# Two packs of weighted values behind one another in every second score step of an attention kernel

## The chip, the core and the metric

The kernel runs on one core of a Trainium2 chip. Five engines work side by side and meet through semaphores: TensorE (PE in the profile; its weight loads are listed apart as PEld), VectorE (DVE), ScalarE (ACT), GpSimd (POOL) and SyncE (SP), which issues nearly all DMAs here. The metric is the device time of one execution in microseconds. The kernel before takes 1724.98 us (median of 3 runs, 1724.56 to 1728.42).

## What is computed

Eight batches, each with 512 query rows of 256 values, attend to a context of 1601 rows (16 heads of 16 values), and then pass a gated feed-forward net whose inputs and weights are rounded blockwise to a four-bit format.

```python
def attention(query, key, value):             # per batch: query 512 x 256, key = value 1601 x 256
    q = split_heads(query @ Wq.T + bq)        # 16 heads of 16
    k = split_heads(key @ Wk.T + bk)
    v = split_heads(value @ Wv.T + bv)
    attn = softmax(einsum('bhqd,bhkd->bhqk', q, k) / sqrt(16))
    return merge_heads(einsum('bhqk,bhkd->bhqd', attn, v)) @ Wo.T + bo
x = x + attention(layernorm(x), ctx, ctx)
xn = layernorm(x)
h = silu(fp4(xn) @ fp4(w_gate).T) * (fp4(xn) @ fp4(w_up).T)      # 704 wide
x = x + fp4(h) @ fp4(w_down).T
```

## The kernel before

The program is one long pipeline over the batches. An iteration computes the attention of one batch (part "att"), the projections and row maxima of the next batch ("early"), the feed-forward net of the batch before ("late"), and loads for the one after that ("next"). There is a prologue, a "first" iteration without a late part, six "loop" iterations, a "last" iteration without an early part, and a tail that holds only a late part.

An iteration has 52 steps: 4 groups of 4 heads times 13 tiles of up to 128 context rows. Step n computes, for the four heads of its group, the scores of one context tile against all 512 queries. The order on every engine is written out by hand, and every engine runs its own list in order. On TensorE a step is, in this order:

- the scores of heads 0 and 1 (`scores(n, 0)`, L837, tile `st`): two bf16 matmuls of 512 columns;
- one "shared" job from the table SLOTS, in the bank `misc`: v (values of a context tile, L720, with the transposes of a tile of the next context, L808), k and q (projections of keys and queries, L713 and L699), o (output projection, L799), xnT, xqT and hqT (transposes), gate and up (L758), down0 and down (L771 and L779). In a loop iteration every step has one;
- the scores of heads 2 and 3;
- two pairs of products of queries and keys for the row maxima (L856, tile `mx`, on 48 of the array's rows each), which VectorE reduces (L1120);
- in some steps a second job (nm, xqT or hqT);
- the weighted values of the step before (`weighted(n - 1)`, L871, tile `pvb`): four fp32 products with 32 columns of weights each, one per head, next to each other in the array. The trace has two rows for each, so a pack is eight rows, in two rounds of four.

ScalarE turns the scores into softmax weights, in the same order: the exponentials of heads 0 and 1 (L1042, tile `prob`), what its engine has to do for the shared job (copying v and the context tile, biases of k or q, tanh for gate, the copies of the transposes), the exponentials of heads 2 and 3, and the copy of a second job.

Three limits matter for the change. Scores have two PSUM banks in a loop iteration: heads 0 and 2 use one, heads 1 and 3 the other. So a score of head 0 of step n+1 waits until the exponential of head 2 of step n has read its bank, and head 1 waits for head 3 (`exp_done2` and `exp_done3`; the class ScoreBanks). In a first or last iteration, steps without a shared job use `misc` as a third bank, and the last one has two more from step 35 on. `prob` has two places, used by turns, so the exponentials of step n wait until `weighted(n - 2)` is done (`pv_done`). And the accumulation in `pvb` runs over the 13 steps of a group; ScalarE then copies it to `pvs` (L1047) at the end of steps 13, 26 and 39 and of step 0 of the next iteration.

Of the kernel before, what the change touches and what calls it, by code (L numbers as in the profile page):

```python
# [5 lines left out]
BF16 = mybir.dt.bfloat16  # L6
# [9 lines left out]
NKT = 13  # L16
# [5 lines left out]
HG = 4  # L22
# [185 lines left out]
LINKS = {"early": 13, "late": 43}  # L208


class Iteration:


# [60 lines left out]
def xattn_ffn(nc, x, ctx_in, wqT, wkT, wvT, woT, bq, bk, bv, bo, w_gate, w_up, w_down, out, scr_k, scr_q):  # L274
    es = ExitStack()
    with es:
# [19 lines left out]
        kp = cin[:, 0:3 * TP // 2].bitcast(BF16).rearrange("p (a n) -> p a n", a=3)  # L296
        kx = [cin[:, 3 * TP // 2 + 402 * j:3 * TP // 2 + 402 * j + 401] for j in range(2)]
        ctxT = sb("ctxT", [128, NC2, TP])
        qp = sb("qp", [128, 3, S], BF16)
        qx = sb("qx", [128, S])  # L300
        kstack = sb("kstack", [ROWS, H, TP], BF16)
        qstack = sb("qstack", [ROWS, H, S], BF16)


        vv = sb("vv", [128, NKT, H // 2, 3 * D])
        vpart = vv[:, :, :, :].rearrange("p t a (b d) -> p t a b d", b=3)
        prob = sb("prob", [128, 2, HG, S])
        xn = sb("xn", [128, QT, E])
        x1 = sb("x1", [128, QT, E])

# [9 lines left out]
        pvs = sb("pvs", [128, S])  # L320
        ht = sb("ht", [128, QT, I])

        mt = sb("mt", [128, QT * E])
        xnT = mt[:, :].rearrange("p (c n) -> p c n", c=NC2)
        hqT = sb("hqT", [128, NF, 128])

        th = [xn[:, :, :].rearrange("p t n -> p (t n)")[:, IH * j:IH * (j + 1)] for j in range(2)]
        st6, mv = sb("st6", [128, QT, 6]), sb("mv", [128, QT, 2])
# [106 lines left out]
        def score_bank(it, n, h):  # L435
            b = SCORES.bank[it.kind, n, h]
            return st[:, b, :] if b < 2 else misc[:, :] if b == 2 else mx[:, 0, b - 3, :]

        def rows_rounding(it, k):

# [192 lines left out]
        def _(pe):  # L633
# [12 lines left out]
            def body(it):  # L646
# [212 lines left out]
                def weighted(n, part):  # L859
                    g, kt = divmod(n, NKT)  # L860
                    w = KROWS[kt]
                    if kt == 0:
                        need(pe, pvs_done, it.count(part, NG, g))
                    if it.kind == "first" and n == 0:
                        pe.wait_ge(s_ones, 1)
                    if n == 0 or 8 <= n < NKT:
                        pe.wait_ge(free["v"], it.count(part, NKT, n + 1 if n else 8))

                    pe.wait_ge(exp_done[HG - 1], it.count(part, STEPS, n + 1))
                    for h in range(HG):  # L870
                        last = mm(pvb[2 * D * h:2 * D * (h + 1), :], vv[0:w, kt, (HG * g + h) // 2, D * (h % 2):D * (h % 2 + 2)], prob[0:w, n % 2, h, :], start=(kt == 0), stop=(kt == NKT - 1))  # L871
                    last.then_inc(pv_done, 1)

                has_att, has_late = "att" in it.parts, "late" in it.parts
# [2 lines left out]
                for n in range(STEPS):  # L877
                    if has_att:
                        scores(n, 0)
                    for job in jobs(it, n, 0):  # L880
                        shared(job)
                    products = maxima(it, n)

                    between = 1 if has_att and not jobs(it, n, 0) else 0
                    for job in products[:between]:
                        pair_products(job)
                    if has_att:
                        scores(n, 1)
                    for job in products[between:2]:
                        pair_products(job)  # L890
                    for job in jobs(it, n, 1):
                        shared(job)
                    if n and has_att:
                        weighted(n - 1, "att")
                    elif n == 0 and has_late:
                        weighted(STEPS - 1, "late")
                    for job in products[2:]:
                        pair_products(job)
# [3 lines left out]
        def _(act):  # L902
# [22 lines left out]
            def body(it):  # L925
                def take(job):
# [24 lines left out]
                    elif kind == "q":  # L951
                        need(act, q_out, c(32, 16 * j))
                        if it.kind == "pre":
                            act.wait_ge(s_wk, 6 * 16)
                        activate(qx[:, :], src, ACT.Identity, bias=bqk[:, 0, j:j + 1])
                        last = activate(qp[:, 0, :], src, ACT.Identity, bias=bqk[:, 0, j:j + 1])
                    elif kind == "k":
                        m, n = divmod(j, 4)
# [13 lines left out]
                    elif kind == "nm":  # L972
                        need(act, nmp_ready, c(NG, j))
                        last = copy(nmf[:, :], src[0:HG * QT, 0:128])
                    elif kind == "xqT":
                        last = copy(rowsT[:, :, 256 * j:256 * (j + 1)], src.rearrange("p (c n) -> p c n", c=NC2))
                    elif kind == "gate":

# [57 lines left out]
                def exps(n, pair):  # L1036
                    kt = n % NKT
                    if pair == 0:
                        need(act, pv_done, it.count("att", STEPS, n - 1))
                    for h in range(2):  # L1040
                        act.wait_ge(st_full, it.count("att", HG * STEPS, HG * n + 2 * pair + h + 1))
                        activate(prob[0:KROWS[kt], n % 2, 2 * pair + h, :], score_bank(it, n, 2 * pair + h)[0:KROWS[kt], :], ACT.Exp, scale=SCALE).then_inc(exp_done[2 * pair + h], 1)  # L1042

                def group_out(g, part):
                    act.wait_ge(pv_done, it.count(part, STEPS, NKT * (g + 1)))
# [38 lines left out]
        def _(dve):  # L1084
# [13 lines left out]
            def body(it):  # L1098
# [30 lines left out]
                def take(job):  # L1129
# [16 lines left out]
                    elif kind == "gate":  # L1146
                        t, half = divmod(j, 2)
                        dve.wait_ge(tanh_done, c(2 * QT, j + 1))
                        v.scalar_tensor_tensor(ht[:, t, half * IH:(half + 1) * IH], th[j % 2], 1.0, src[:, 0:IH], op0=ALU.add, op1=ALU.mult).then_inc(free["gate"], 1)  # L1149
                    elif kind == "up":  # L1150
                        t, half = divmod(j, 2)
# [192 lines left out]
        def _(pool):  # L1344
# [43 lines left out]
            def body(it):  # L1388
# [8 lines left out]
                def work(part, what, k):  # L1397
# [11 lines left out]
                        last.then_inc(xb_ready, 1)  # L1409
                    elif what == "q":  # L1410
                        pool.wait_ge(free["q"], c(2, k + 1))
                        split(qx[:, :], qp, q_step, lambda n: c(4, 2 * k + n), q_split)
                    elif what == "k":

                        m, n = divmod(k, 4)
# [81 lines left out]
```

## Time and profile before

| | |
|---|---|
| device time, median of 3 runs | 1724.98 us |
| the profiled execution | 1726.32 us |
| its span, first to last instruction | 1724.5 us |
| TensorE busy | 1653.4 us, 96% |
| VectorE busy | 1427.4 us, 83% |
| ScalarE busy | 1132.4 us, 66% |
| GpSimd busy | 553.3 us, 32% |
| exponentials on ScalarE (L1042) | 1591 in `st` and 73 in other banks, 599 ns each |
| weighted values on TensorE (L871) | 3328 rows, 606 ns each, 444.2 us |
| TensorE's scores waiting for exponentials, whole run | 2.4 us, 10 waits |
| mean granted clock of TensorE | 0.991 of full |
| a loop iteration, six of them | 202.3 us |

The busy time of TensorE counts a matmul from its start to its modelled end. Matmuls overlap, so the distance of one start to the next says what a matmul costs, and a short wait between two starts can hide in the busy time of the one before. Where a row of the timeline holds several instructions ("x2"), it gives the start of the first and the time to the end of the last.

### The profile page before, as it was taken

The page shows a single profiled execution, that of the slowest core. Times are in us where ns is not written, and L with a number is a line of the kernel's source. Part 1 is how long each engine was busy: PE and PEld are TensorE (multiplying, and loading weights), DVE is VectorE, ACT ScalarE, POOL GpSimd, SP SyncE. Part 2 cuts the span into 40 slices and gives each one's busy share as a digit, 9 for nine tenths or more (in the row PEclk, how much of TensorE's full clock was granted, in tenths as well). Part 3 has the DMA queues.
Part 4 walks back from the last instruction along what each step waited for, and adds up shares of the span by engine and source line. Part 5 has one row for each costly group of instructions (what it writes and reads, how often), then busy time and mean ns, then how long its engine had stood idle before and what let it go on. Part 6 is the DMA issues. An engine that isn't in the chain of part 4 may idle for free.

```text
span 1724.5 us, 27130 instructions
## 1 busy us (share of the span) xinstructions
PE 1653.4 (96%) x9496; PEld 666.1 (39%) x9496; DVE 1427.4 (83%) x2078; ACT 1132.4 (66%) x2295; POOL 553.3 (32%) x667
## 2 busy tenths in 40 slices
PE   6899899999999999999999999999999999989978
PEld 4332234333433344333443334333443334323345
DVE  5878988988798978898889887898879887898447
ACT  3377677766777667776677667776677766666731
POOL 5238520732025320443107321263303431013303
PEclk9899999999999999999999999999999999999989
DMA  6745332431235332142323323254222323200000
GB/s 166 158 81 136 70 70 45 97 98 36 57 59 118 74 63 55 49 116 48 78 45 77 105 43 60 45 120 86 52 53 60 81 48 67 44 8 10 13 22 13
DMA packets 106771, 117.53 MB, mean 68 GB/s; under 512 B 23236, under 2 KB 88140, under 8 KB 106636
## 3 DMA queue, kind: packets, MB, share of 16 engines
q1 hardware_dynamic: 101808, 111.62, 30.7%
q10 hardware_dynamic: 4828, 4.18, 1.0%
q8 instruction: 76, 1.25, 0.3%
q14 instruction: 59, 0.48, 0.1%
HBM read 76.78 MB, written 30.16 MB: 62 GB/s over the span
## 4 chain that ended last, share of the span: by engine, by line
PE 82%; DVE 11%; ACT 4%; issue 2%; DMA 1%; POOL 0%; ACTq 0%; SPq 0%; DVEq 0%
PE pvb L871 21%; PE st L837 20%; PE mx L856 10%; PE misc L758 7%; DVE cmx L1120 5%; PE misc L720 5%; PE misc L713 4%; PE misc L779 3%; ACT prob L1042 2%; PE misc L771 2%; PE misc L699 2%; PE misc L767 1%; PE misc L799 1%; PE misc L808 1%; DVE ht L1149 1%
## 5 line engine op out<-in xcount | busy, mean ns | idle before, releaser
L1042 ACT ACTIVATE prob<-st 128x512 f32<-128x512 f32 (+1 forms) x1591 | 867.6, 599 | 374.7 <-PE st L837 371.2
L1120 DVE TENSOR_REDUCE cmx<-mx 128x2 f32<-128x1024 f32 x768 | 904.9, 1219 | 150.5 <-PE mx L856 145.4
L837 PE MATMUL st<-qstack,kstack 112*128 112x512 bf16 (+1 forms) x1591 | 496.9, 384 | 8.5 <-ACT prob L1042 2.4
L871 PE MATMUL pvb<-prob,vv 128*32 128x512 f32 (+1 forms) x3328 | 444.2, 606 | 0.6 <-ACT prob L1042 0.6
L837 PEld LDWEIGHTS st<-qstack,kstack 112*128 112x128 bf16 (+1 forms) x1591 | 128.1, 98 | 463.4 <-issue 236.4
L856 PE MATMUL mx<-kstack,qstack 48*128 48x512 bf16 (+1 forms) x2048 | 256.8, 336 | 18.4 <-DVE cmx L1120 18.0
L1385 POOL TENSOR_TENSOR ht<-ht,rh 128x352 f32<-128x352 f32 (+1 forms) x78 | 56.9, 751 | 418.1 <-DVE rh L1096 418.1
L758 PE MATMUL misc<-wguT,rowsT 128*128 128x352 f32 x456 | 153.7, 458 | 0.0
L1377 POOL TENSOR_TENSOR ht<-ht,mt 128x352 f32<-128x352 f32 (+1 forms) x136 | 120.8, 911 | 69.5 <-DVE mt L1283 60.1
L856 PEld LDWEIGHTS mx<-kstack,qstack 48*128 48x128 bf16 x2048 | 59.8, 94 | 199.7 <-issue 138.0
L1391 POOL TENSOR_TENSOR cin<-cin 128x400 f32<-128x400 f32 (+1 forms) x60 | 55.7, 928 | 250.6 <-ACT cin L967 250.6
L871 PEld LDWEIGHTS pvb<-prob,vv 128*32 128x32 f32 (+1 forms) x3328 | 65.7, 108 | 132.3 <-issue 120.3
L1408 POOL TENSOR_TENSOR x<-x,bob 128x256 f32<-128x256 f32 x32 | 22.3, 733 | 287.1 <-issue 271.1
L758 PEld LDWEIGHTS misc<-wguT,rowsT 128*128 128x128 f32 x456 | 86.4, 190 | 40.9
L720 PE MATMUL misc<-wv,ctxT 128*128 128x256 f32 (+1 forms) x392 | 101.8, 382 | 0.0
L713 PE MATMUL misc<-ctxT,wk 128*128 128x400 f32 (+1 forms) x236 | 89.3, 500 | 0.0
L720 PEld LDWEIGHTS misc<-wv,ctxT 128*128 128x128 f32 (+1 forms) x392 | 73.0, 187 | 21.1 <-issue 0.5
L1185 DVE RECIPROCAL sums<-sums 128x128 f32<-128x128 f32 x64 | 60.3, 941 | 17.4 <-DMA sums<-pvs 17.4
L1385 POOL TENSOR_TENSOR ht<-ht,sh 128x352 f32<-128x352 f32 (+1 forms) x80 | 60.4, 777 | 2.8
L1377 POOL TENSOR_TENSOR xa<-xa,ht 128x256 f32<-128x256 f32 x56 | 39.5, 726 | 66.2 <-DVE ht L1237 65.1
L1395 POOL TENSOR_TENSOR cin<-cin 128x400 bf16<-128x400 f32 (+1 forms) x60 | 58.7, 978 | 4.7
L966 ACT ACTIVATE cin<-misc,bqk 128x400 f32<-128x400 f32 (+1 forms) x59 | 35.1, 595 | 28.0 <-PE misc L713 25.5
(192 smaller groups left out, 1558.5 us busy)
## 6 DMA issues: line engine op xcount, KB each, us to landing
kstack<-scr_k SPq DMA_DIRECT2D x378, 100.1 KB, 4.4
scr_k<-cin SPq DMA_DIRECT2D x48, 300.0 KB, 4.1
qstack<-scr_q SPq DMA_DIRECT2D x372, 32.0 KB, 1.9
cin<-ctx_in SPq DMA_DIRECT2D x16, 512.0 KB, 5.4
scr_q<-qp SPq DMA_DIRECT2D x16, 384.0 KB, 4.3
scr_k<-cin SPq DMA_DIRECT2D x16, 300.8 KB, 4.8
xn<-x SPq DMA_DIRECT2D x8, 512.0 KB, 3.9
cin<-ctx_in SPq DMA_DIRECT2D x16, 256.0 KB, 5.6
```

Source lines behind the costliest of these rows:

```text
L713: last = mm(o[:, 0:w], wk[:, h, m * 128:(m + 1) * 128], ctxT[:, h, COFF[n]:COFF[n] + w], start=(h == 0), stop=(h == NC2 - 1))
L720: last = mm(o[0:w, 0:E], ctxT[:, h, KOFF[j]:KOFF[j] + w], wv[:, h, :], start=(h == 0), stop=(h == NC2 - 1))
L758: last = mm(o[:, 0:IH], rowsT[:, h, t * 128:(t + 1) * 128], wguT[:, h, first:first + IH], start=(h == 0), stop=(h == NC2 - 1))
L837: mm(score_bank(it, n, h)[0:KROWS[kt], :], kstack[:, hd, KOFF[kt]:KOFF[kt] + KROWS[kt]], qstack[:, hd, :], start=True, stop=True).then_inc ...
L856: last = mm(mx[:, q % 2, par, at:at + w], qstack[r0:r0 + LEAD, hd, t * 128:(t + 1) * 128], kstack[r0:r0 + LEAD, hd, k0:k0 + w], start=True ...
L871: last = mm(pvb[2 * D * h:2 * D * (h + 1), :], vv[0:w, kt, (HG * g + h) // 2, D * (h % 2):D * (h % 2 + 2)], prob[0:w, n % 2, h, :], start= ...
L1042: activate(prob[0:KROWS[kt], n % 2, 2 * pair + h, :], score_bank(it, n, 2 * pair + h)[0:KROWS[kt], :], ACT.Exp, scale=SCALE).then_inc(exp_ ...
L1120: v.tensor_reduce(cmx[:, g % 2, h0:h0 + 2, at:at + 1], products, op=ALU.max, axis=AX.X).then_inc(max_free, 1)
L1185: v.reciprocal(sums[:, cols], sums[:, cols]).then_inc(rec_ready, 1)
L1377: last = g_.tensor_tensor(out[:, cols], in0[:, cols], in1[:, cols], op)
L1385: last = g_.tensor_tensor(part, part, over(sc[:, j * w:(j + 1) * w]), ALU.mult)
L1395: g_.tensor_tensor(parts[:, 2, :], whole, parts[:, 1, :], ALU.subtract).then_inc(done, 1)
```

## The change

The weighted values move. `weighted_behind(n)` says which steps' packs stand at the end of step n: none in an even step, those of steps n-2 and n-1 one behind the other in an odd step. Steps 0, 1, 26 and 27 keep one pack each, so an iteration has 24 pairs of an even step without a pack and an odd step with two. `prob` gets a third place, chosen by a count that runs through the whole program, and the exponentials wait for `pv_done` one step further back. To make room, three buffers lose their own memory: `qx` (the queries before they are split into bf16 parts) goes to `rowsT` or `x1`, `qp` (the parts) into `ht`, and `hqT` into `xa`. Two waits protect them: ScalarE's copy for xqT waits for the split of the queries (`q_split`), and VectorE's work on gate 4 waits until the parts have been written out (`q_out`).

```diff
+def weighted_behind(n):
+    if n in (1, 2 * NKT, 2 * NKT + 1):
+        return [n - 1]
+    return [n - 2, n - 1] if n % 2 and n > 1 else []
...
-        qp = sb("qp", [128, 3, S], BF16)
-        qx = sb("qx", [128, S])
...
-        prob = sb("prob", [128, 2, HG, S])
+        prob = sb("prob", [128, 3, HG, S])
...
+        qp = ht[:, :, :].rearrange("p t n -> p (t n)")[:, 2048:2816].bitcast(BF16).rearrange("p (a n) -> p a n", a=3)
...
-        hqT = sb("hqT", [128, NF, 128])
+        hqT = xa[:, 0:NF * 128].rearrange("p (f n) -> p f n", f=NF)
...
+        def queries_whole(it):
+            return x1[:, 0:2, :].rearrange("p t n -> p (t n)") if it.kind in ("pre", "first") else rowsT[:, 1, :]
+
+        def probs(it, part, n):
+            return prob[:, (it.batch(part) * STEPS + n) % 3, :, :]
...
-                    if n and has_att:
-                        weighted(n - 1, "att")
-                    elif n == 0 and has_late:
+                    for m in weighted_behind(n) if has_att else []:
+                        weighted(m, "att")
+                    if n == 0 and has_late:
                         weighted(STEPS - 1, "late")
...
                     elif kind == "xqT":
+                        if "early" in it.parts:
+                            act.wait_ge(q_split, it.count("early", 2, 2))
...
                     if pair == 0:
-                        need(act, pv_done, it.count("att", STEPS, n - 1))
+                        need(act, pv_done, it.count("att", STEPS, n - 2))
...
                     elif kind == "gate":
                         t, half = divmod(j, 2)
                         dve.wait_ge(tanh_done, c(2 * QT, j + 1))
+                        if j == 4 and "early" in it.parts:
+                            dve.wait_ge(q_out, it.count("early", 32, 32))
```

On TensorE, at the end of step 48 of the fourth loop iteration (`st` scores, `mx` products for the maxima, `pvb` weighted values, `misc` the shared job v), the order before is this.

```order
L856 MATMUL mx<-kstack,qstack 128x512 [waits max_free]
L856 MATMUL mx<-kstack,qstack 128x512
L871 MATMUL pvb<-prob,vv 32x512 [waits exp_done3]
L871 MATMUL pvb<-prob,vv 32x512 x3
L837 MATMUL st<-qstack,kstack 128x512 [waits exp_done2]
L837 MATMUL st<-qstack,kstack 128x512 [waits exp_done3]
L720 MATMUL misc<-wv,ctxT 128x256 [waits ctxT_free,v_free]
```

A pack stands between the last products of the step and the first scores of the next. At the same place the order is now this.

```order
L873 MATMUL mx<-kstack,qstack 128x512 [waits max_free]
L873 MATMUL mx<-kstack,qstack 128x512
L854 MATMUL st<-qstack,kstack 128x512 [waits exp_done2]
L854 MATMUL st<-qstack,kstack 128x512 [waits exp_done3]
L737 MATMUL misc<-wv,ctxT 128x256 [waits ctxT_free,v_free]
```

The scores of step 49, with the same waits for the exponentials of step 48, follow the products directly. At the end of step 49 TensorE has this order now.

```order
L873 MATMUL mx<-kstack,qstack 128x512 [waits max_free]
L873 MATMUL mx<-kstack,qstack 128x512
L888 MATMUL pvb<-prob,vv 32x512 [waits exp_done3]
L888 MATMUL pvb<-prob,vv 32x512 x3
L888 MATMUL pvb<-prob,vv 32x512 [waits exp_done3]
L888 MATMUL pvb<-prob,vv 32x512 x3
L854 MATMUL st<-qstack,kstack 128x512 [waits exp_done2]
L854 MATMUL st<-qstack,kstack 128x512 [waits exp_done3]
```

Both packs stand there, one behind the other, where one stood before.

## Rows read from the trace of the kernel before

**Rows 1.** The page: busy time, share of the span, instructions; the granted clock in 40 slices.
```profile
PE 1653.4 (96%) x9496; PEld 666.1 (39%) x9496; DVE 1427.4 (83%) x2078; ACT 1132.4 (66%) x2295; POOL 553.3 (32%) x667
...
PEclk9899999999999999999999999999999999999989
```
**Rows 2.** TensorE's timeline, ends of steps 47 and 48: start, duration, instructions.
```profile
1060.28 0.61 PE L871 MATMUL pvb<-prob,vv 128*32 128x512 f32 x4
1060.82 0.61 PE L837 MATMUL st<-qstack,kstack 112*128 112x512 bf16 x2
...
1063.41 1.07 PE L871 MATMUL pvb<-prob,vv 128*32 128x512 f32 x8
1064.41 0.60 PE L837 MATMUL st<-qstack,kstack 112*128 112x512 bf16 x2
```
**Rows 3.** ScalarE's timeline, last exponentials of step 48 and first of step 49.
```profile
1063.12 1.11 ACT L1042 ACTIVATE prob<-st 128x512 f32<-128x512 f32 x2
1064.90 1.09 ACT L1042 ACTIVATE prob<-st 128x512 f32<-128x512 f32 x2 [0.67 <-PE st L837]
```
**Rows 4.** The chain that ended last, in step 8 (job xnT): start, us, what.
```profile
903.51 0.60 ACT prob L1042
904.11 0.05 issue
904.16 0.39 PE st L837
```
**Rows 5.** TensorE's timeline: packs ending steps 8, 14, 24, 30; scores after 14.
```profile
905.02 1.06 PE L871 MATMUL pvb<-prob,vv 128*32 128x512 f32 x8
...
929.30 1.06 PE L871 MATMUL pvb<-prob,vv 128*32 128x512 f32 x8
930.30 0.73 PE L837 MATMUL st<-qstack,kstack 112*128 112x512 bf16 x2
...
968.52 1.07 PE L871 MATMUL pvb<-prob,vv 128*32 128x512 f32 x8
...
992.35 1.06 PE L871 MATMUL pvb<-prob,vv 128*32 128x512 f32 x8
```
**Rows 6.** ScalarE's timeline: last exponentials of steps 8, 14, 24, 30.
```profile
904.46 1.12 ACT L1042 ACTIVATE prob<-st 128x512 f32<-128x512 f32 x2
...
929.50 1.08 ACT L1042 ACTIVATE prob<-st 128x512 f32<-128x512 f32 x2
...
968.02 1.08 ACT L1042 ACTIVATE prob<-st 128x512 f32<-128x512 f32 x2
...
991.70 1.09 ACT L1042 ACTIVATE prob<-st 128x512 f32<-128x512 f32 x2 [0.88 <-PE st L837]
```
**Rows 7.** TensorE's timeline: the pack ending step 22, the shared job of 23.
```profile
961.14 1.07 PE L871 MATMUL pvb<-prob,vv 128*32 128x512 f32 x8
...
962.59 0.76 PE L758 MATMUL misc<-wguT,rowsT 128*128 128x352 f32 x2
```
**Rows 8.** ScalarE's timeline in step 22: last exponentials, then the copy for xqT.
```profile
959.91 1.09 ACT L1042 ACTIVATE prob<-st 128x512 f32<-128x512 f32 x2 [0.47 <-PE st L837]
961.25 0.58 ACT L976 COPY rowsT<-misc 128x512 f32<-128x512 f32 x1 [0.26 <-PE misc L749]
```
**Rows 9.** Timelines of the split, its DMA, the xqT copy and gate 4.
```profile
937.72 1.17 POOL L1395 TENSOR_TENSOR qp<-qx,qp 128x512 bf16<-128x512 f32 x1
...
948.07 0.59 ACT L976 COPY rowsT<-misc 128x512 f32<-128x512 f32 x1
...
947.63 0.50 SPq L491 DMA_DIRECT2D scr_q<-qp  x1
...
983.50 0.52 DVE L1149 SCALAR_TENSOR_TENSOR ht<-xn,misc 128x352 f32<-128x352 f32 x1 [0.52 <-ACT xn L986]
```
**Rows 10.** First iteration: a stretch (PEclk third from the end) and a pack in it.
```profile
160.00:175.00 15.00, 13.31 (x76) 3.65 (x68) 11.53 (x11) 8.91 (x19) 6.91 (x11) 0.89 0.52 159
...
163.94 1.93 PE L871 MATMUL pvb<-prob,vv 128*32 128x512 f32 x8
```

More of the change, by code:

```diff
@@ L870, in weighted @@
                     for h in range(HG):
-                        last = mm(pvb[2 * D * h:2 * D * (h + 1), :], vv[0:w, kt, (HG * g + h) // 2, D * (h % 2):D * (h % 2 + 2)], prob[0:w, n % 2, h, :], start=(kt == 0), stop=(kt == NKT - 1))
+                        last = mm(pvb[2 * D * h:2 * D * (h + 1), :], vv[0:w, kt, (HG * g + h) // 2, D * (h % 2):D * (h % 2 + 2)], probs(it, part, n)[0:w, h, :], start=(kt == 0), stop=(kt == NKT - 1))
                     last.then_inc(pv_done, 1)
@@ L954, in take @@
                             act.wait_ge(s_wk, 6 * 16)
-                        activate(qx[:, :], src, ACT.Identity, bias=bqk[:, 0, j:j + 1])
+                        activate(queries_whole(it), src, ACT.Identity, bias=bqk[:, 0, j:j + 1])
                         last = activate(qp[:, 0, :], src, ACT.Identity, bias=bqk[:, 0, j:j + 1])
@@ L1038, in exps @@
                     if pair == 0:
-                        need(act, pv_done, it.count("att", STEPS, n - 1))
+                        need(act, pv_done, it.count("att", STEPS, n - 2))
                     for h in range(2):
                         act.wait_ge(st_full, it.count("att", HG * STEPS, HG * n + 2 * pair + h + 1))
-                        activate(prob[0:KROWS[kt], n % 2, 2 * pair + h, :], score_bank(it, n, 2 * pair + h)[0:KROWS[kt], :], ACT.Exp, scale=SCALE).then_inc(exp_done[2 * pair + h], 1)
+                        activate(probs(it, "att", n)[0:KROWS[kt], 2 * pair + h, :], score_bank(it, n, 2 * pair + h)[0:KROWS[kt], :], ACT.Exp, scale=SCALE).then_inc(exp_done[2 * pair + h], 1)
                 def group_out(g, part):
@@ L1411, in work @@
                         pool.wait_ge(free["q"], c(2, k + 1))
-                        split(qx[:, :], qp, q_step, lambda n: c(4, 2 * k + n), q_split)
+                        split(queries_whole(it), qp, q_step, lambda n: c(4, 2 * k + n), q_split)
                     elif what == "k":
```

## The prediction

> **What bounds the kernel now.** The page comes first: TensorE is busy 96% of the span, VectorE 83%, ScalarE 66%, at full clock in nearly all slices [rows 1]. So TensorE sets the time, and an edit is worth what it takes off, or adds to, the distance between TensorE's starts. The second view is TensorE's timeline at the end of a step. A pack of weighted values starts at 1063.41, the scores of the next step at 1064.41: a pack costs 1.00 us of TensorE [rows 2]. Its two rounds are not alike: a second round alone stands 0.54 before the next scores (1060.28 to 1060.82), so a first round takes 0.46. The end of a pack costs 0.08 more than a round that another round follows.
>
> The third view is ScalarE's timeline beside it, since the scores have two banks. In step 8, where little work lies between, the chain of waits shows what this means: an exponential of 0.60 us, 0.05 of issue, and then the score that takes its bank [rows 4]. So the first score of a step can't start before the exponential of head 2 has ended, the second not before that of head 3, plus 0.05 each. In step 48 these two end at 1063.74 and 1064.23 (the row starts at 1063.12, lasts 1.11 and holds two of about 0.62, so the first ends 0.49 before the second) [rows 3]. The scores of step 49 start at 1064.41, after both. The pack is what covers the exponentials. When TensorE reaches the pack, at 1063.41, neither has ended.
>
> **The change part by part.** *The odd step's second pack.* It follows another pack. No row shows a pack after a pack; the nearest is a round after a round, 0.46, so the first of two packs costs 2 x 0.46 = 0.92 before the second starts. Bounds: 2 x 0.43 = 0.86 would be a little less than the rows show for any round; 1.00 is a pack that something else follows. I take 0.92, since a round behind a round is the same kind of instruction on the same columns of the array. The saving over 1.00 is 0.08 for each of 192 pairs (24 in each of 8 iterations), 15 us in all, with nothing else counted.
>
> For this choice the Trainium skill has a rule (TensorEngine Tiling (Array Packing), section Key Properties): changing the tiling mode drains the engine, going to another tile of the same mode does not. By it the second pack starts without a drain, and the sum is the one with 0.92; without it the sum is that of the rival below with 1.00. No run here shows it for two packs.
>
> *The even step without its pack.* Let P be the time at which TensorE has done the products of the step and E2, E3 the ends of the last two exponentials. Before, the second score of the next step starts at P + 1.00 + 0.23. Now it starts at the latest of P + 0.23, E2 + 0.05 + 0.23 and E3 + 0.05. The pair of steps changes by 0.92 minus the time by which this score comes earlier. That the exponentials end where they do in the trace follows from ScalarE's rows: it waits for the scores before its first exponential (0.67 in step 49 [rows 3]), so it carries no lag into a step, and a longer odd step before gives it more time still. In an odd step the shift of the second score pushes the job by the same amount, which the score's start already holds; two packs of 1.92 us then cover its own exponentials.
>
> - Jobs v (step 48): E3 + 0.05 = 1064.28 against 1064.64 before, 0.36 earlier; 0.92 - 0.36 = +0.56.
> - Jobs k and q (step 14): P = 929.30, E3 = 929.50 + 1.08 = 930.58, because ScalarE first has two biases to do [rows 5, 6]. The second score comes at 930.63; before it came at 930.30 + 0.23 + 0.13 = 930.66, since the row of the two scores is 0.73 long where others are 0.60, so the wait stood there already. Hardly anything is won: +0.89. Steps 12 and 16, whose own scores started 0.2 late before and no longer will, +0.71.
> - xnT (step 8): P = 905.02, E3 = 905.58; 905.63 against 906.25: +0.30 [rows 5, 6].
> - gate (step 24): P = 968.52, E3 = 969.10; 969.15 against 969.75: +0.32. down (step 30): P = 992.35, E3 = 992.79; 992.84 against 993.58: +0.18 [rows 5, 6].
> - Steps with a second job (22): P = 961.14, E3 = 961.00 [rows 7, 8]. The exponentials are covered, the scores come 1.00 earlier, -0.08. But the job of step 23 needs the bank that ScalarE empties until 961.25 + 0.58 = 961.83. It stood at 962.59, 1.45 after P, so it could start at 961.59, and waits until 961.88: +0.29. Together +0.21.
>
> The 24 pairs of a loop iteration, by even step: v 2, 42, 48, 50 at 0.56, 4 (a tile of 65 rows) 0.44, 44 (with hqT) 0.27, in all 2.95. k and q 14 at 0.89, 12 and 16 at 0.71, 18 (xqT next) 0.54, 10 (with nm) 0.43, in all 3.28. xnT 6 and 8: 0.60. gate 20 and 24: 0.42 + 0.32. down 30 and 36 at 0.18, 40 and 46 at 0.28: 0.92. Second jobs 22 and 32 at 0.21, 28 and 38 at about 0.06, 34 at -0.08: 0.46. Sum: 8.95 us on an iteration of 202.3 us. Six loop iterations: +54. In the first and last iterations many steps have no job and more banks, so the wait is milder. I take one loop's 9 for the two together, between 0 and 18.
>
> *The third place in `prob`.* It takes a wait away that ended nothing: the exponentials wait for scores, which stand behind the pack on TensorE's own list. Its price is nothing, but without it the exponentials would wait for the moved pack.
>
> *The shared buffers.* The xqT copy waits for the split, which ends at 938.89, 9 us before the copy at 948.07. Gate 4 waits for a DMA issued at 947.63 and needs it at 983.50 [rows 9]. Behind the first wait stand ScalarE's exponentials, behind the second VectorE's reductions, but 9 and 36 us of cover do not go away when steps get 0.4 us longer.
>
> *VectorE.* In an odd step the products come up to 1.0 us earlier against the reductions. VectorE has had the 0.92 of the odd step before to catch up, and no less time per pair than now, so I count nothing.
>
> The sum: 1726.3 of the profiled execution + 54 + 9 = 1789.3; that execution lay 1.3 above the median, so **1788 us**, 3.7% slower.
>
> **The rivals.** *The scores do not wait (faster).* If the score after the products found its bank free, only the saving of the shape would be left: 192 x -0.08 = -15, 1710 us. For it: TensorE's list of waits shows 2.4 us behind exponentials in the whole run (the table of the profile), as if ScalarE were never late. Against it: that is the state with the pack in between, and the order of the change keeps the waits for heads 2 and 3 on the scores that now follow the products. It would decide if the exponentials of an even step ended before P in most of the 24 pairs; the rows have that in 5. Chance 6%.
>
> *No difference.* The waits would have to be a fourth of what the rows give, so that 0.08 a pair pays for them, for instance because ScalarE ran ahead in even steps. It can't run ahead of the scores it waits for. 1725 us, 4%. That the change does not do what it says is excluded by the order.
>
> *The second pack drains as well.* 192 x 0.08 more: 1803 us. Nothing in the rows speaks for it but the absence of such a row. 12%.
>
> *The clock falls.* The first iteration has one stretch with a mean granted clock of 0.89 [rows 10], where TensorE had waited for VectorE; in it the clock was at its lower level, 1.2 of 2.4 GHz, for a while, and a pack lasted 1.93 us instead of 1.07. If each step whose new wait is near 1 us (12, 14, 16, 18) cost one such pack, 0.86 us, that would be 6 x 4 x 0.86 = 21 us: 1809 us. Against it: the clock stands at full in the slices of the loop iterations [rows 1], and the new waits lie between stretches of 2 us and more of dense work. 4%. The Trainium skill names such a case (TensorE: Matmul & The Clock Gate, section A second HAM failure mode: psum-queue depth-cycling): short, frequent idle spells between groups of matmuls that rotate PSUM banks let the clock swing between its levels. By it the time would be this rival's; the loop iterations before, with short waits in some steps, do not show it.
>
> **How the numbers follow.** Forecast 74%, two packs with a drain 12%, clock 4%, no difference 4%, faster 6%. The likeliest is 1788. Its own bounds: first and last iterations 9 less or more, the first pack at 0.86 instead of 0.92 (192 x 0.06 = 12 less). Terms of the loop that I sized from one step of a kind may be off by a tenth, 5. That gives 1762 at the low end, and 1802 above; with the drain 1803 and something of the ends 1810. So 1762 to 1810, which leaves out the faster case, no difference and most of the clock's. A measurement of this kernel tells about 0.3% from no change: faster 0.06, same 0.04, slower 0.90.
>
> **What would show it.** In the changed profile TensorE's list of waits must have a large row of scores behind exponentials, at the ends of even steps; v steps must show the two scores 0.49 apart instead of 0.23; two packs must take about 1.92 us from first start to next scores; a loop iteration must last about 211 us. I am wrong if scores follow the products at once in v or k steps, or if ScalarE's last exponentials end earlier against P than above.

## The result and the profile after

The changed kernel takes **1794.67 us** (median of 4 runs, 1793.87 to 1796.89), the kernel before, run beside it, 1726.52 us (1724.56 to 1728.42). The ratio is 1.0397, with a 95% interval of 1.0384 to 1.0410: 4% slower. The forecast was 1788, between 1762 and 1810.

The page of the changed kernel, with the lines that answer to [rows 1], the start of the chain of waits (shares of the span by engine), and from the table of groups the line of the scores (operation, count, busy us and mean ns, then the idle time before it and what ended it); under it, the same line from the page of the kernel before. L854, L873, L888 and L1062 are now the scores, the products, the weighted values and the exponentials.

```profile
PE 1665.0 (93%) x9496; PEld 687.5 (38%) x9496; DVE 1424.2 (79%) x2078; ACT 1128.5 (63%) x2295; POOL 555.9 (31%) x667
...
PEclk9999899999999999999999999999999999999999
...
PE 69%; ACT 13%; DVE 13%; issue 3%; DMA 1%; POOL 1%; ACTq 0%; SPq 0%; DVEq 0%
...
L854 PE MATMUL st<-qstack,kstack 112*128 112x512 bf16 (+1 forms) x1591 | 516.5, 385 | 51.4 <-ACT prob L1062 32.5
```

```profile
L837 PE MATMUL st<-qstack,kstack 112*128 112x512 bf16 (+1 forms) x1591 | 496.9, 384 | 8.5 <-ACT prob L1042 2.4
```

The granted clock is 0.989 of full, 0.991 before. TensorE's share fell from 96% to 93%, ScalarE's in the chain rose from 4% to 13%, and the scores wait 32.5 us for exponentials where they waited 2.4. Those two figures hold the longer waits alone. All idle time ahead of the scores rose from 8.5 to 51.4 us, and their busy time from 496.9 to 516.5, because the two scores of a pair overlap less when the second waits too. Together the two grew by 62.5 us; the span grew by 68.

TensorE's timeline of the changed kernel, end of step 48 of the fourth loop iteration, step 49, and the start of step 50 (start, duration, instructions; in brackets the idle time and what ended it). It answers to [rows 2].

```profile
1109.08 0.60 PE L873 MATMUL mx<-kstack,qstack 48*128 48x512 bf16 x4
1110.00 0.88 PE L854 MATMUL st<-qstack,kstack 112*128 112x512 bf16 x2 [0.31 <-ACT prob L1062]
...
1112.33 0.61 PE L873 MATMUL mx<-kstack,qstack 48*128 48x512 bf16 x4
1112.86 1.93 PE L888 MATMUL pvb<-prob,vv 128*32 128x512 f32 x16
1114.72 0.61 PE L854 MATMUL st<-qstack,kstack 112*128 112x512 bf16 x2
```

The products of step 48 started at 1109.08; in step 49 what follows the products starts 0.53 behind them (1112.33 to 1112.86), so TensorE was free at 1109.61 and the first score came 0.39 later, at 1110.00. The row of the two scores lasts 0.88 instead of 0.60: the second waited too. Both packs take 1.86 us from start to the next scores (1112.86 to 1114.72), not the forecast's 1.92. ScalarE's timeline beside it holds the exponentials for which the scores waited, as in [rows 3].

```profile
1109.33 2.24 ACT L1062 ACTIVATE prob<-st 128x512 f32<-128x512 f32 x4
...
1112.57 1.11 ACT L1062 ACTIVATE prob<-st 128x512 f32<-128x512 f32 x2
```

The first row holds the last two exponentials of step 48 and, with hardly a gap, the first two of step 49. In an even step nothing stands between them any more. The table by iteration (stretch: length, then each engine's busy time; the number behind POOL's is the granted clock) shows where the time lies: the first iteration, the first loop iteration, the sixth, and the last with the tail.

```profile
71.10:276.79 205.69, 185.00 (x1078) 65.64 (x1079) 164.04 (x204) 136.88 (x281) 83.64 (x110) 0.96 0.41 84
276.79:488.16 211.37, 201.75 (x1174) 82.60 (x1171) 173.61 (x253) 140.43 (x286) 64.40 (x74) 1.00 0.32 67
...
1333.80:1542.39 208.59, 200.09 (x1159) 80.75 (x1155) 168.99 (x228) 138.22 (x278) 64.40 (x74) 1.00 0.28 58
1542.39:1792.60 250.21, 223.23 (x1215) 101.16 (x1211) 172.46 (x293) 131.11 (x267) 51.80 (x62) 0.97 0.09 19
```

Before, the same four lasted 195.9, 202.3, 201.5 and 245.5 us. So the first iteration lost 9.8, each of the first five of the loop 9.0 (8.9 to 9.1), the sixth 7.1, and the last with the tail 4.7; the first scores came 1.5 later. That makes 68.1, which is the difference of the spans (1724.5 to 1792.6).

### The profile page after: what moved, and what is told of

Its sections match the earlier page's. It is cut to its first block, busy times and chain, and to the rows that moved or that the text cites. A ratio compares the mean times of both kernels' runs of the same rounds, so it can differ in the third digit from the quotient of the medians.

```text
span 1792.6 us, 27141 instructions
## 1 busy us (share of the span) xinstructions
PE 1665.0 (93%) x9496; PEld 687.5 (38%) x9496; DVE 1424.2 (79%) x2078; ACT 1128.5 (63%) x2295; POOL 555.9 (31%) x667
## 4 chain that ended last, share of the span: by engine, by line
PE 69%; ACT 13%; DVE 13%; issue 3%; DMA 1%; POOL 1%; ACTq 0%; SPq 0%; DVEq 0%
PE pvb L888 20%; PE st L854 15%; ACT prob L1062 8%; DVE cmx L1140 7%; PE mx L873 7%; PE misc L775 6%; PE misc L737 5%; PE misc L730 4%; PE misc L796 2%; PE misc L788 2%; PE misc L716 1%; PE misc L784 1%; PE misc L816 1%; ACT cin L983 1%; ACT cin L984 1%
## 5 line engine op out<-in xcount | busy, mean ns | idle before, releaser
L1062 ACT ACTIVATE prob<-st 128x512 f32<-128x512 f32 (+1 forms) x1591 | 867.9, 600 | 404.6 <-PE st L854 396.5
L854 PE MATMUL st<-qstack,kstack 112*128 112x512 bf16 (+1 forms) x1591 | 516.5, 385 | 51.4 <-ACT prob L1062 32.5
L888 PE MATMUL pvb<-prob,vv 128*32 128x512 f32 (+1 forms) x3328 | 408.1, 605 | 0.1
L854 PEld LDWEIGHTS st<-qstack,kstack 112*128 112x128 bf16 (+1 forms) x1591 | 136.8, 98 | 440.9 <-issue 210.2
L873 PE MATMUL mx<-kstack,qstack 48*128 48x512 bf16 (+1 forms) x2048 | 255.7, 336 | 21.2 <-DVE cmx L1140 20.9
L888 PEld LDWEIGHTS pvb<-prob,vv 128*32 128x32 f32 (+1 forms) x3328 | 85.9, 110 | 193.8 <-issue 165.2
L873 PEld LDWEIGHTS mx<-kstack,qstack 48*128 48x128 bf16 x2048 | 59.1, 94 | 200.8 <-issue 124.0
L1180 DVE SCALAR_TENSOR_TENSOR ht<-misc,ht 128x352 f32<-128x352 f32 x56 | 29.3, 523 | 39.1 <-PE misc L775 39.1
```

What stands on the lines that cost most here:

```text
L854: mm(score_bank(it, n, h)[0:KROWS[kt], :], kstack[:, hd, KOFF[kt]:KOFF[kt] + KROWS[kt]], qstack[:, hd, :], start=True, stop=True).then_inc ...
L873: last = mm(mx[:, q % 2, par, at:at + w], qstack[r0:r0 + LEAD, hd, t * 128:(t + 1) * 128], kstack[r0:r0 + LEAD, hd, k0:k0 + w], start=True ...
L1062: activate(probs(it, "att", n)[0:KROWS[kt], 2 * pair + h, :], score_bank(it, n, 2 * pair + h)[0:KROWS[kt], :], ACT.Exp, scale=SCALE).then_ ...
```

## The experiments

The theory is that of the prediction: the pack covered the exponentials, and the next scores now wait for their two banks. Against it stood the shared buffers, the third place and the added waits; VectorE; and the shared bank `misc`.

**One pack at the end of each step, all else as changed.**

```diff
-    if n in (1, 2 * NKT, 2 * NKT + 1):
-        return [n - 1]
-    return [n - 2, n - 1] if n % 2 and n > 1 else []
+    return [n - 1] if n else []
```

> The changed kernel with one part undone: every step again has the pack of the step before, while the third place for the weights, the shared buffers and the two added waits stay. Theory (the loss is the scores' wait for the exponentials of an even step, which the moved pack no longer covers): back to the kernel before, 1725 us, within 3. Rival (a good part of the loss comes from the shared buffers, the added waits or the third place): between 1740 and 1795.

Measured: 1726.07 us, ratio to the kernel before 1.0003 (0.9993 to 1.0012). Its list of waits on TensorE has the 2.4 us back.

```profile
PE st L852 <- ACT prob L1060: 2.4, 10, 0.3
```

Loop iterations agree with those before to 0.1 us. The shared buffers, the third place and the two new waits cost nothing that this run can show; the loss comes from the order of the packs.

**Exponentials of half the queries, with one pack and with pairs.** The edit on the changed kernel; the other run has the same in the kernel with one pack:

```diff
-    activate(probs(...)[0:KROWS[kt], 2 * pair + h, :], score_bank(...)[0:KROWS[kt], :], ACT.Exp, scale=SCALE)
+    activate(probs(...)[0:KROWS[kt], 2 * pair + h, 0:S // 2], score_bank(...)[0:KROWS[kt], 0:S // 2], ACT.Exp, scale=SCALE)
```

> As the kernel with one pack behind every step, but each exponential does 256 of the 512 queries, and the weights of the others stay at one; the weighted values read all 512 as before. It is the base for the next run. An exponential should take some 0.33 us instead of 0.60. TensorE waits little for ScalarE here even now, so by either theory 1700 to 1722 us.

> The same halved exponentials (256 of 512 queries, the other weights stay at one) with the packs in pairs as in the change. Theory: the two last exponentials of an even step now end before or soon after the products, the wait is gone in most even steps and only the saving is left, 0.12 us for each of 192 pairs by the trace after, so 10 to 23 us faster than the run with one pack. Rival (the loss lies in the pairs themselves, or in buffers): 50 to 70 us slower than the run with one pack.

Measured: 1713.94 us with one pack (ratio 0.9934, 0.9919 to 0.9948) and 1746.88 with pairs (1.0129, 1.0112 to 1.0146). The pairs are still 33 us slower, not faster: 4.0 us per loop iteration instead of 9.0. That expectation was wrong. TensorE's timeline with pairs, end of step 14 (job k), and of step 48 (job v):

```profile
941.89 0.67 PE L854 MATMUL st<-qstack,kstack 112*128 112x512 bf16 x2 [0.57 <-ACT prob L1062]
...
1077.03 0.60 PE L873 MATMUL mx<-kstack,qstack 48*128 48x512 bf16 x4
1077.73 0.67 PE L854 MATMUL st<-qstack,kstack 112*128 112x512 bf16 x2
```

And ScalarE's in the same two places, with the two biases of the k job ahead of the first exponentials:

```profile
940.48 0.60 ACT L983 ACTIVATE cin<-misc,bqk 128x401 f32<-128x401 f32 x1 [0.71 <-PE misc L730]
940.97 0.59 ACT L984 ACTIVATE cin<-misc,bqk 128x401 bf16<-128x401 f32 x1
941.45 0.66 ACT L1062 ACTIVATE prob<-st 128x256 f32<-128x256 f32 x2
...
1077.28 0.68 ACT L1062 ACTIVATE prob<-st 128x256 f32<-128x256 f32 x2
```

In step 14 two half exponentials take 0.66, the second starting 0.28 behind the first, so one takes 0.38. The first ends at 941.45 + 0.38 = 941.83, and the score comes at 941.89, 0.06 later. In step 48 the two take 0.68, so one takes 0.40: the first ends at 1077.68 and the score comes at 1077.73. So the scores do follow the end of the exponential by 0.05 to 0.06 here too. What I had wrong is how much earlier that end would come: the two biases of a k step are as long as before and hold the exponentials up, and half an exponential is more than half as long (0.38 of 0.60). The v pairs fell from +0.52 to +0.09, the k pairs 12 to 16 kept +0.46 to +0.87, and pairs 32 and 36 kept +0.60 and +0.63, so that these two wait for something else.

**Four banks for the scores.** Half of the products and their reductions are left out, and the two banks so won hold the scores of every other pair of heads, with one pack and with pairs:

```diff
-    banks = [0, 1] + [2] * (kind != "loop" and not any(step)) + [3, 4] * (kind == "last" and n >= WIDE)
+    banks = [0, 1, 5, 6] + [2] * (kind != "loop" and not any(step)) + [3, 4] * (kind == "last" and n >= WIDE)
...
-                found.append((part, q, g, j, 2 * pair, piece))
+                if q % 2 == 0:
+                    found.append((part, q, g, j, 2 * pair, piece))
```

> One pack behind every step, with the shared buffers and the third place. Every second product for the row maxima and its reduction is left out, so that the products need two PSUM banks instead of four, and the scores have the two others: four banks, used in turn. The maxima are then over half of the tiles and zero. Base for the next run: TensorE loses one product of 0.22 to 0.27 us per step, so some 1610 to 1650 us.

> The same (half of the products and reductions left out, four banks for scores) with the packs in pairs as in the change. The exponentials are as long as before. Theory: a score now waits for the exponential of the same head one step earlier, long done, so the wait of the even steps is gone and the saving of 0.12 us a pair is left, less where the one buffer of the products waits for VectorE: 8 to 23 us faster than the run with one pack. Rival (ScalarE's total work, not the bank, makes the pairs slow): 40 to 70 us slower than the run with one pack.

Measured: 1625.88 us with one pack (0.9414, 0.9396 to 0.9431), 1632.62 with pairs (0.9458, 0.9441 to 0.9475). The loss is down to 6.7 us, 0.5 per loop iteration, but it is no gain: the expected 8 to 23 us in favour of the pairs were wrong. TensorE's timeline with one pack, end of step 48:

```profile
1002.25 0.39 PE L872 MATMUL mx<-kstack,qstack 48*128 48x512 bf16 x2
1002.57 1.07 PE L887 MATMUL pvb<-prob,vv 128*32 128x512 f32 x8
1003.57 0.60 PE L853 MATMUL mx<-qstack,kstack 112*128 112x512 bf16 x2
```

With pairs, in step 19 (the scores of heads 2 and 3), in step 33, at the end of step 48 and at the end of step 49:

```profile
892.78 0.87 PE L855 MATMUL st<-qstack,kstack 112*128 112x512 bf16 x2
...
944.69 1.45 PE L776 MATMUL misc<-wguT,rowsT 128*128 128x352 f32 x4 [0.24 <-ACT xa L1015]
...
1004.59 0.39 PE L874 MATMUL mx<-kstack,qstack 48*128 48x512 bf16 x2
1004.92 0.60 PE L855 MATMUL mx<-qstack,kstack 112*128 112x512 bf16 x2
...
1007.29 1.93 PE L889 MATMUL pvb<-prob,vv 128*32 128x512 f32 x16
1009.15 0.39 PE L855 MATMUL mx<-qstack,kstack 112*128 112x512 bf16 x1
```

With their banks free, the scores of step 49 start 0.33 behind the products of step 48, and their row is 0.60 long: neither waits. Two packs take 1.86 against twice 1.00, and the v pairs 2, 4, 48 and 50 and the down pairs 30, 36, 40 and 46 gain the whole 0.14. What is left is in other pairs: 10, 14, 18, 22, 28, 32, 38 and 44 lose 0.10 to 0.39. The row of step 33 shows what most of them wait for: its job needs the bank `misc`, which ScalarE is still emptying of the second job of step 32 (the copy to `xa`). The pack had covered that copy as well. Six of the seven even steps with a second job (10, 22, 28, 32, 38, 44, all but 34) are among them, and in the odd step behind each the job starts 0.67 to 0.96 after the step's first score, where with one pack it starts at 0.44. Pair 14 looks the same in kind: the job of step 15 comes 0.14 later than with one pack, 0.05 behind the end of the bias with which ScalarE empties `misc` of the job of step 14. Pair 18 is still a wait for a score's bank: in step 19 the two scores of heads 2 and 3 last 0.87 instead of 0.60, since the second waits for the exponential of head 3 of step 18, which the k job's biases delay. That `misc` holds the others up is read from these rows; no run gave it a second bank.

**More work in the steps, even or odd.** The second pair of products is done twice in ten steps of each loop iteration, some 0.22 us each, 13 us in all; once in even steps, once in the odd steps behind them. The changed kernel ran beside them once more.

```diff
-                        pair_products(job)
+                        pair_products(job, it.kind == "loop" and n in (2, 4, 10, 12, 16, 18, 20, 42, 48, 50) and job is products[1])
```

> The changed kernel once more, as the base of the next three on the same chip: 1795 us, 3.9 to 4.1% above the kernel before.

> The changed kernel with work added: in ten even steps of each loop iteration (2, 4, 10, 12, 16, 18, 20, 42, 48, 50) TensorE does the second pair of products twice, with the same result, 0.22 us more in 60 places, 13 us of work. Theory: in these steps the scores that follow wait at least as long for the exponentials, so the added work falls into the wait: 0 to 2 us slower than the changed kernel. Rival (TensorE is the bound there): 13 us slower.

> The same added work in the ten odd steps that follow (3, 5, 11, 13, 17, 19, 21, 43, 49, 51), ahead of the two packs. Both theories have TensorE as the bound there: 11 to 14 us slower than the changed kernel. It is the control for the run before.

Measured: the changed kernel 1794.22 us (1792.93 to 1796.26); work added in even steps 1794.02 (1793.56 to 1794.97); in odd steps 1805.66 (1804.21 to 1806.73). Thirteen microseconds of TensorE's work are free in one place and cost 11.4 one step later. TensorE's timeline at the end of step 48 with the work in the even step:

```profile
1109.46 0.82 PE L873 MATMUL mx<-kstack,qstack 48*128 48x512 bf16 x6
1110.38 0.88 PE L854 MATMUL st<-qstack,kstack 112*128 112x512 bf16 x2
```

The products are six instead of four, and the scores start 0.92 behind them, exactly as in the changed kernel (1109.08 to 1110.00). In those ten pairs of the first five loop iterations the difference is 0.00. In an odd step the same work stays:

```profile
1121.60 0.82 PE L873 MATMUL mx<-kstack,qstack 48*128 48x512 bf16 x6
1122.35 1.92 PE L888 MATMUL pvb<-prob,vv 128*32 128x512 f32 x16
```

Here the packs follow 0.75 behind the products instead of 0.53, and nine of the ten pairs are 0.21 to 0.22 longer. The tenth, pair 20, stayed as it was: the second job of step 21 had waited 0.21 us for VectorE's `ht`, and the added work fell into that wait. So the end of these even steps is a wait that does not depend on when TensorE gets there.

**VectorE's other work moved.** Pairs 32 and 36 lost 0.60 and 0.63 where the forecast had 0.21 and 0.18. TensorE's timeline of the changed kernel, hqT in step 33 and then step 37, and VectorE's beside step 37:

```profile
1047.30 0.44 PE L784 MATMUL misc<-ident,ht 128*128 128x128 f32 x2 [0.26 <-DVE ht L1180]
...
1062.98 0.61 PE L873 MATMUL mx<-kstack,qstack 48*128 48x512 bf16 x4
1064.28 0.66 PE L784 MATMUL misc<-ident,ht 128*128 128x128 f32 x4 [0.70 <-DVE ht L1172]
1064.87 1.92 PE L888 MATMUL pvb<-prob,vv 128*32 128x512 f32 x16
```

```profile
1062.71 0.20 DVE L1196 CAST nmp<-nmf 16x128 bf16<-16x128 f32 x1
1062.95 0.28 DVE L1197 TENSOR_TENSOR nmr<-nmf,nmp 16x128 f32<-16x128 f32 x1
1063.27 0.21 DVE L1198 CAST nmp<-nmr 16x128 bf16<-16x128 f32 x1
1063.52 0.28 DVE L1199 TENSOR_TENSOR nmp<-nmr,nmp 16x128 bf16<-16x128 f32 x1
1063.73 0.50 DVE L1172 SCALAR_TENSOR_TENSOR ht<-xn,misc 128x352 f32<-128x352 f32 x1
```

The second job of step 37, hqT, needs `ht`, which VectorE makes behind the four conversions of nm. Both packs stand behind hqT. In step 33 VectorE makes `ht` behind a reciprocal of 0.94 us for the attention's values. In the first run the place of three items in VectorE's plan was changed; in the second nm goes the other way:

```diff
-    ... 32: [("att", "values", 2)], ... 36: [("att", "nm", 3)], 38: [("att", "values", 3)], ...
+    ... 35: [("att", "nm", 3)], 38: [("att", "values", 2)], ... 41: [("att", "values", 3)],
```

```diff
+    ... 37: [("att", "nm", 3)], 38: [("att", "values", 2)], ... 41: [("att", "values", 3)],
```

> The changed kernel with two pieces of VectorE's small work at other steps: the second and third division of the attention's values from 32 to 38 and from 38 to 41, and the splitting of the maxima of group 3 from step 36 to 35. Theory for the two pairs that cost more than forecast (32 and 36: +0.60 and +0.63 measured, +0.21 and +0.18 forecast): the second job of the odd step waits for VectorE, which is held up by this small work and so empties the job's bank late. Moved, 0.3 to 0.9 us per loop iteration come back, 2 to 5 us in all. Rival (those steps wait for GpSimd's rounding or for ScalarE): no difference to the changed kernel, or slower.

> The order of VectorE's other work as in the run before with `values` moved (values 2 from step 32 to 38, values 3 from 38 to 41), but the four conversions of nm 3 go the other way, from step 36 to step 37, so that on VectorE's list they stand behind the reductions of step 37 and behind the gate product (ht), not ahead of them. In the changed kernel these conversions took VectorE from 2.16 to 3.24 us after the start of step 37, and the hqT job of step 37 began at 3.73, just behind ht (3.17 to 3.67). Theory (VectorE's other work stands ahead of ht in the odd step, and hqT waits for it): ht starts about 0.9 earlier, hqT follows the products at about 3.0 to 3.3, and the pair 36 loses 0.4 to 0.6 of its +0.63; the pair 32 keeps the 0.33 that moving values 2 gave. Some 0.8 to 0.9 us per loop iteration against the changed kernel, 5 to 7 us in all: about 1788. Rival (hqT of step 37 waits for the shared bank or for the gate job itself, whatever VectorE does): the pair 36 stays at +0.6 and the time at that of the run before, 1793. If the conversions come too late for the queries' transfer of step 39, the scores of step 39 start late and the gain is lost there.

Measured: 1792.98 us (1790.72 to 1798.33) for the first, which can't be told from the 1794.22 beside it. Pair 32 lost 0.33 of its 0.60 in every loop iteration, so there the cause is shown. Pair 36 got 0.04 to 0.05 longer. VectorE's timeline of that run, step 36 and the start of 37:

```profile
1055.01 0.81 DVE L1196 CAST nmp<-nmf 16x128 bf16<-16x128 f32 x1
1055.85 0.92 DVE L1197 TENSOR_TENSOR nmr<-nmf,nmp 16x128 f32<-16x128 f32 x1
1056.80 0.76 DVE L1198 CAST nmp<-nmr 16x128 bf16<-16x128 f32 x1
1057.60 0.77 DVE L1199 TENSOR_TENSOR nmp<-nmr,nmp 16x128 bf16<-16x128 f32 x1
1058.30 0.40 DVE L1182 TENSOR_TENSOR x<-x,misc 128x256 f32<-128x256 f32 x1
```

The conversions took three to four times as long as in step 37, and the emptying of `misc` (L1182) came behind them, so that the next gate job was late instead. GpSimd's timeline in the same stretch:

```profile
1053.80 2.82 POOL L1400 TENSOR_TENSOR ht<-ht,mt 128x352 f32<-128x352 f32 x3
1056.70 1.53 POOL L1408 TENSOR_TENSOR ht<-ht,sh 128x352 f32<-128x352 f32 x2
```

With nm behind `ht`: 1797.86 us (1796.43 to 1798.99; ratio to the kernel before 1.0414, 1.0397 to 1.0431), where 1788 was expected: no faster than the changed kernel, and by the medians 3 us slower, though the intervals of the two ratios overlap. In each loop iteration pair 32 lost 0.33 and pair 36 lost 0.49, as the theory has it. But pair 38 got 0.44 longer, and that of the first iteration 6.6. The list of waits on TensorE in that run (us in total, times, the longest) has a row that says why; in the changed kernel it is 0.3 us, once:

```profile
PE st L854 <- DMA qstack<-nmp: 9.7, 8, 5.2
```

The transfer of nm's result into `qstack` now lands after the scores of step 39 could start; that was the miss named in the expectation, and in the first iteration it cost more than all the rest gave. The cause of most of the excess of pairs 32 and 36 is shown, and a cure without a new wait was not found.

## Why the prediction was right, and where it was off

*What bounds, and what the pack covered: right.* One pack with all else changed gives the old time, free banks (with half of the reductions gone as well) take away most of the loss, and work put into ten of the even steps vanishes in their waits.

*The formula for the scores: right.* For step 48 it asks for the first score at E2 + 0.05 and the second 0.49 later. ScalarE's row gives E2: it starts at 1109.33, and its first exponential takes 0.61, so E2 is 1109.94. The first score came at 1110.00, 0.06 later, the second (0.88 is the row of both, less 0.39 for one) 0.49 behind it. By the distances of the steps' first scores, the v pairs were forecast at +0.56 and measured at +0.52, xnT +0.30 and +0.26, gate 20 and 24 +0.42 and +0.32 against +0.37 and +0.27, k 14 +0.89 against +0.86. Only 12 (+0.71, measured +0.51) was off by more than 0.1 among the steps without a second job and without the VectorE waits below. The prediction had sized the second scores; by these 12 agrees (+0.70), while 14 is +0.66 against +0.89 and 16 +0.83 against +0.71, with the same sum over the iteration: which k pair gets what depends on where one cuts.

*The second pack behind the first: mis-sized.* I took 0.92 for the first pack, 1.92 for both. Measured are 1.86 for both, the lower of the two bounds, so a pair without waits saves 0.14, not 0.08; the runs with four banks show just this 0.14. Over 192 pairs that is, as an estimate, 192 x 0.06 = 11.5 us to the good of the change. The rival that the second pack drains the engine is out. The Trainium skill's rule (TensorEngine Tiling (Array Packing), section Key Properties), by which changing the tiling mode drains TensorE and another tile of the same mode does not, agrees with these 1.86 us.

*VectorE counted at nothing: wrong.* The step was "VectorE has had the 0.92 of the odd step before to catch up". It looked at reductions against products, and left out that the second job of an odd step waits for VectorE's *other* work. Since the scores behind the even step come up to a microsecond sooner, hqT in steps 33 and 37 now meets it: +0.39 and +0.45 more than forecast on pairs 32 and 36, 0.84 per iteration, of which moving that work gave back 0.33 + 0.49. By luck it cancels the rest: the differences of the other 22 pairs sum to -0.77, so that 8.95 forecast stand against 9.0 measured. The smaller pack alone would have made them 22 x -0.06 = -1.32, so other terms, those of second jobs most of all, were some 0.55 too low as well.

*`misc`.* The term for second jobs (+0.21 for pair 22, measured +0.27) was of the right kind, and the runs with four banks show that it would be the bound if the scores' banks were not. With half of the reductions gone there too, the 8.5 us of a loop iteration that four banks take away hold VectorE's 0.8; some 7.7, as an estimate, are the scores' banks.

*The sixth iteration counted in full: wrong by 1.8.* It still has its v jobs, but there is no batch behind the next one whose context tiles it would transpose: 10 transposes instead of 26, and 5 copies of them on ScalarE instead of 13. In its v steps 42, 48 and 50 the exponentials come earlier for that, and the pairs cost nothing (-0.01 to 0.01).

*First and last iterations, 9 together, between 0 and 18: 14.5.* The first alone lost 9.8. In it TensorE's listed waits for exponentials rose from 2.4 to 5.2 us and those for VectorE's reductions, which I had counted at nothing, from 7.3 to 10.6. Part of the loss is the clock, the fourth rival in one place. The stretch from 188 to 198 us, in the changed kernel and in the one before (granted clock behind POOL's busy time):

```profile
188.00:198.00 10.00, 8.06 (x32) 1.55 (x31) 9.83 (x12) 3.85 (x9) 8.52 (x14) 0.66 0.33 83
```

```profile
188.00:198.00 10.00, 8.50 (x54) 2.64 (x54) 9.89 (x12) 5.93 (x12) 4.71 (x8) 1.00 0.93 137
```

TensorE's timeline in it, changed and before:

```profile
190.44 0.61 PE L873 MATMUL mx<-kstack,qstack 48*128 48x512 bf16 x2 [1.94 <-DVE cmx L1140]
...
192.48 3.64 PE L888 MATMUL pvb<-prob,vv 128*32 128x512 f32 x16
```

```profile
188.53 0.39 PE L856 MATMUL mx<-kstack,qstack 48*128 48x512 bf16 x2 [2.04 <-DVE cmx L1120]
```

In the changed kernel TensorE had stood idle 1.94 us for VectorE's reduction. Then the clock was at its lower level, 1.2 of 2.4 GHz, and the two packs took 3.64 us instead of 1.93. But the kernel before stood idle 2.04 us at almost the same place, for a reduction of VectorE too, and there the clock stayed at 1.00. So that spell alone does not make the clock fall, and what does stays open. Over the whole first iteration the granted clock is 0.96, before 0.98. From these two figures and the iterations' lengths I estimate that the clock explains at most some 4 of the 9.8 us. In the loop iterations it is 1.00: their waits at the end of even steps, up to 0.85 us ahead of the first score and 0.26 more ahead of the second, did not move it, and that rival was rightly set low. The Trainium skill's case of frequent short idle spells between groups that rotate PSUM banks (TensorE: Matmul & The Clock Gate, section A second HAM failure mode: psum-queue depth-cycling) did not come about in these iterations; the measurement decides.

*The sum.* 1789.3 was forecast for the profiled execution, whose span grew by 68.1 where I had 63: loops 52.2 (forecast 53.7), first and last 14.5 (9), the start 1.5 (0). In the runs of the changed order with work added to it or moved in it, and in its repeat, the first scores stood between 69.8 and 71.2, before at 69.6, so part of the last term varies from run to run; whether the change has a share in it stays open.

## What to carry to other kernels

Before a block of work is moved off the end of a step, ask what it covers: for every bank or buffer that the work behind it needs, take the time at which its last reader ends, add the measured delay from that end to the next instruction (0.05 us here), and compare it with the time at which the engine would now arrive. Do this for all such readers, the shared bank and the second jobs' inputs too, since with the first wait gone the pairs still lost 6.7 us to the next. And to see whether a place is a wait, put work there: what costs 13 us of an engine and moves the time by nothing lies in a wait.

## What the runs showed of the hardware

A pack of weighted values behind another is 0.14 us cheaper than one behind other matmuls (1.86 for two against 2 x 1.00).

An exponential of 128x256 takes 0.38 to 0.40 us where one of 128x512 takes 0.60, and the next starts after 0.28 instead of 0.49: half the columns are not half the time.

VectorE's four conversions on 16 partitions took 0.20, 0.28, 0.21 and 0.28 us while GpSimd was idle, and 0.81, 0.92, 0.76 and 0.77 while it ran additions and multiplications of 0.8 to 0.9 us. The Trainium skill (SBUF — State Buffer, section SBUF: two separate sides) says that GpSimd and a VectorE instruction with two inputs in SBUF, or in a mode that uses two ports, share a pair of ports, which the one that starts first holds for its whole instruction; the trace agrees in that each conversion ended 0.08 to 0.15 us behind the end of a GpSimd instruction that had started ahead of it. That this lock is the cause was not tested by a run of its own, and no run shows in which mode the two casts among the four ran.
